# Layer 4's edges by tiles, and layer 3's node normalization three chunks ahead, in a four-layer graph network kernel

## The reference

```
# layer 3 (L2): message passing
h        = swish(concat(node[src], node[dst], edge_attr_32) @ We1 + be1)
agg      = segment_sum(h @ We2 + be2, dst) / 16
agg      = layernorm(agg) * g_msg + b_msg
nf       = swish(concat(node, agg) @ Wn1 + bn1) @ Wn2 + bn2
out      = layernorm(node + nf) * g_node + b_node

# layer 4 (L3): continuous filter convolution
C   = 0.5 * (cos(edge_weight * pi / 10) + 1)
W   = (ssp(edge_attr_50 @ mlp_w1.T + mlp_b1) @ mlp_w2.T + mlp_b2) * C[:, None]
msg = (x @ lin1_w.T)[src] * W
agg = segment_sum(msg, dst)
out = ssp(agg @ lin2_w.T + lin2_b)          # ssp(v) = softplus(v) - log 2
```

## Time and profile before

| | us |
|---|---|
| median of three runs | 9322.11 |
| profiled execution | 9326.77 |
| its span | 9325.0 |
| layer 3's edges, in the span | 4911 to 6950 |
| layer 3's nodes | 6950 to 7167 |
| layer 4's table | 7167 to 7213 |
| layer 4's edges | 7213 to 9277 |
| layer 4's nodes | 9277 to 9325 |

### The profile page before, as it was taken

The page is one execution under the profiler, slowest core; times in us unless marked ns, Lnnn a source line. Parts: engine busy times, 40 slices in busy tenths (PEclk is TensorE's granted clock), DMA queues, the critical chain, the costliest instruction groups (busy, mean ns, idle before and its releaser), DMA issues. The chain is left out here.

```text
span 9325.0 us, 221484 instructions
## 1 busy us (share of the span) xinstructions
PE 8295.5 (89%) x54969; PEld 6586.8 (71%) x54970; DVE 5838.0 (63%) x12428; ACT 5420.3 (58%) x14197; POOL 4943.9 (53%) x5229
## 2 busy tenths in 40 slices
PE   5999999989897999989988888888885999999998
PEld 4888888888884777766656666666663666666666
DVE  6888888888885777751145555555554555555555
ACT  5777777777774444430026767676754555555555
POOL 5666666666660000000007777777760777777775
PEclk8999999999998999999989999999997999999999
DMA  6888888888881222235544444444430222222222
GB/s 193 224 227 226 227 224 227 226 226 227 225 226 43 111 110 117 110 125 192 190 143 116 118 118 118 118 118 118 118 112 28 74 73 73 73 73 73 73 73 69
DMA packets 963534, 1294.60 MB, mean 139 GB/s; under 512 B 187018, under 2 KB 821186, under 8 KB 934210
## 3 DMA queue, kind: packets, MB, share of 16 engines
q1 hardware_dynamic: 769858, 837.45, 30.7%
q0 software_dynamic: 193536, 455.41, 17.7%
HBM read 906.61 MB, written 385.62 MB: 139 GB/s over the span
## 5 line engine op out<-in xcount | busy, mean ns | idle before, releaser
L1823 POOL DMA_INDIRECT x<-table,p_gidx x1632 | 1546.5, 948 | 2377.7 <-ACT p_gidx L1860 1957.9
L672 POOL DMA_INDIRECT g_G<-table,g_runs x1776 | 1686.5, 950 | 769.9 <-issue 479.5
L2275 POOL DMA_INDIRECT c_G<-table,c_gidx x1632 | 1548.4, 949 | 505.2 <-issue 497.1
L820 PE MATMUL g_ps_cell<-g_loh,g_kw 128*98 128x128 f32 x9472 | 1254.1, 277 | 29.2 <-DVE g_kw L743 29.2
L831 PE MATMUL g_ps_rev<-g_hrow,g_AT 128*128 128x129 f32 x7252 | 1054.6, 284 | 192.3 <-DMA g_AT<-turn_save 155.1
L820 PEld LDWEIGHTS g_ps_cell<-g_loh,g_kw 128*98 128x98 f32 x9472 | 1127.5, 168 | 29.7 <-DVE g_kw L743 29.4
L1913 PE MATMUL p_ps_sum<-x 128*96 128x256 f32 x3264 | 898.4, 398 | 231.5 <-DVE hid L1849 221.3
L798 ACT COPY g_X<-g_ps_cell 98x512 f32<-98x512 f32 x1184 | 681.4, 576 | 720.8 <-PE g_ps_cell L820 697.9
L831 PEld LDWEIGHTS g_ps_rev<-g_hrow,g_AT 128*128 128x128 f32 x7252 | 930.2, 197 | 239.9 <-issue 184.0
L1913 PEld LDWEIGHTS p_ps_sum<-x 128*96 128x96 f32 x3264 | 468.7, 163 | 646.0 <-ACT x L1878 260.3
L1849 DVE TENSOR_TENSOR hid<-hid,p_ps_sum 96x256 f32 x1632 | 678.0, 415 | 375.2 <-DVE hid L1849 372.1
(11 more groups left out here) (344 smaller groups left out, 15168.1 us busy)
## 6 DMA issues: line engine op xcount, KB each, us to landing
turn_save<-g_X SPq DMA_DIRECT2D x1184, 196.0 KB
g_AT<-turn_save SPq DMA_DIRECT2D x592, 392.0 KB
adj_save<-a_A SPq DMA_DIRECT2D x74, 1568.0 KB, 5.1
a_A<-adj_save SPq DMA_DIRECT2D x74, 1568.0 KB, 6.6
c_ed<-in_edge_dram SPq DMA_DIRECT2D x1632, 25.0 KB
g_G<-table,g_runs POOLq DMA_INDIRECT x1776
p_lhs<-in_edge_dram SPq DMA_DIRECT2D x1632, 16.0 KB
x<-table,p_gidx POOLq DMA_INDIRECT x1632
```

Of the source, the lines that this page charges most:

```text
L672: g.indirect_dma_start(G[:, e % GR, q, 0:D], None, table, bass.IndirectOffsetOnAxis(ap=runs[:, n % 2, 0, RQ * e + q:RQ * e + q + 1], axis= ...
L820: last = pe.matmul(ps_cell[q % 2][0:KEYS, r * P:(r + 1) * P], kw[:, b, cell, :], loh[:, b, cell, :], start=True, stop=True)
L1823: g.indirect_dma_start(G[:, H * b + q, :], None, table2, bass.IndirectOffsetOnAxis(ap=gidx[:, b, q:q + 1], axis=0)).then_inc(gathered[b], 16)
L2275: g.indirect_dma_start(G[:, H * b + q, :], None, table, bass.IndirectOffsetOnAxis(ap=gidx[:, b, q:q + 1], axis=0)).then_inc(gathered[b], 16)
```

## The change

In layer 4's edges the loop over pairs becomes straight-line code over 391 steps of four tiles, followed by sums of pairs: every tile is loaded, filtered and gathered once, in the order of the tiles, and only one-hots, sums and adds still go over 408 quads of pairs. The source indices come from a new input `src_cols` in one transfer of 128 x 1564 integers. `c_G` becomes a ring of 32 steps, from which PE picks a pair's tile at a slot that it computes in registers (`slots_of`). The one-hots are made up to 17 steps ahead, between the adds. The bias is cut into three bf16 parts and put into `c_ps_filt` by a bf16 product. ACT's three copies, the `top` matrix and the loop's bookkeeping go; `c_ps_filt` and `c_ps_sum` get three banks instead of two. The sums of step n wait for the messages of tile step min(n, 390).

In layer 3's nodes ACT's take_aggT and activate, and DVE's take_nf and measure_nf, come three chunks later in their streams (`LEAD`).

```diff
+LEAD = 3
+STEPS = NI * NB
+TSTEPS = -(-ET // H)
+RS = 32
+CES = 4
+COH = 18
...
-                        for c in range(NQ + 4):
+                        for c in range(NQ + 4 + LEAD):
...
-                            if 3 <= c < NQ + 3:
-                                take_nf(c - 3)
-                            if c >= 4:
-                                measure_nf(c - 4)
+                            if 3 + LEAD <= c < NQ + 3 + LEAD:
+                                take_nf(c - 3 - LEAD)
+                            if c >= 4 + LEAD:
+                                measure_nf(c - 4 - LEAD)
...
-                            if 1 <= c <= NQ:
-                                take_aggT(c - 1)
-                            if c >= 2:
-                                activate(c - 2)
+                            if 1 + LEAD <= c <= NQ + LEAD:
+                                take_aggT(c - 1 - LEAD)
+                            if c >= 2 + LEAD:
+                                activate(c - 2 - LEAD)
...
+                def slots_of(eng, n):
+
+                    word = eng.value_load(bucket_row[0:1, bass.ds(n, 1)])
+                    return [nc.s_assert_within(eng.snap((n * H + q + 2 * P - ((word >> (7 * q)) & 127)) & (RS * H - 1)), 0, RS * H - 1,
+                                               skip_runtime_bounds_check_because="masked to the ring") for q in range(H)]
...
+                        sp.dma_start(index[:, :], a["src_cols"]).then_inc(index_in, 16)
...
+                        for s in range(TSTEPS):
+                            if s >= CES:
+                                sp.wait_ge(linear, s - CES + 1)
+                            sp.dma_start(ed[0:DE3, s % CES, :], a["edge50"][:, s * CH:(s + 1) * CH]).then_inc(edges_in[s % CES], 16)
...
+                        for s in range(TSTEPS):
+
+                            if s >= RS:
+                                g.wait_ge(summed, (H * (s - RS) + H - 1 + NBK - 1) // H + 1)
                             for q in range(H):
-                                g.indirect_dma_start(G[:, H * b + q, :], None, table,
-                                                     bass.IndirectOffsetOnAxis(ap=gidx[:, b, q:q + 1], axis=0)).then_inc(gathered[b], 16)
...
+                                g.indirect_dma_start(G[:, s % RS * H + q, :], None, table,
+                                                     bass.IndirectOffsetOnAxis(ap=index[:, H * s + q:H * s + q + 1], axis=0)).then_inc(gathered[s % RS], 16)
...
+                        for n in range(STEPS + 2):
+                            bucket = buckets_of(v, n - 2) if n >= 2 else None
+                            if n < TSTEPS:
+                                messages(n)
+                            ahead = min(2 * n + 3, n + COH - 1, STEPS)
                             for q in range(H):
...
+                                if n >= 2:
+                                    add_up(n - 2, q, bucket)
+                                for m in range(made, ahead):
+                                    one_hot(m, q)
+                            made = ahead
...
+                        def filters(s):
+                            if s >= 3:
+                                pe.wait_ge(message, s - 2)
+                            pe.matmul(ps_filt[s % 3][:, :], one[:, :], shift[:, :, :].rearrange("p q d -> p (q d)"), start=True, stop=False)
+                            pe.wait_ge(act_step, 4 * s + 4)
...
+                        def make_sums(n, slot):
+                            if n >= 3:
+                                pe.wait_ge(added, H * (n - 2))
+                            pe.wait_ge(oh_ready, n + 1)
+                            pe.wait_ge(message, tile_step(n) + 1)
...
+                        line(0)
+                        for n in range(STEPS + 1):
+                            if n + 1 < TSTEPS:
+                                line(n + 1)
+                            slot = slots_of(pe, n - 1) if n >= 1 else None
+                            if n < TSTEPS:
+                                filters(n)
+                            if n >= 1:
+                                make_sums(n - 1, slot)
```

More of the change, by code:

```diff
@@ new lines, in messages, with add_up @@
+                        def messages(s):
+                            v.wait_ge(filtered, s + 1)
+                            v.wait_ge(gathered[s % RS], 16 * H * (s // RS + 1))
+                            here = G[:, s % RS * H:(s % RS + 1) * H, :]
+                            v.tensor_tensor(here, here, by_tile(ps_filt[s % 3][:, :]), ALU.mult).then_inc(message, 1)
+                        def add_up(n, q, bucket):
+                            at = bass.ds(bucket[q], 1)
+                            if q == 0:
+                                v.wait_ge(summed, n + 1)
+                            if n or q:
+                                v.wait_ge(added, H * n + q)
+                            v.tensor_tensor(acc[0:BN, at, :], acc[0:BN, at, :],
+                                            ps_sum[n % 3][0:BN, q * P:(q + 1) * P].rearrange("p (o d) -> p o d", o=1),
+                                            ALU.add).then_inc(added, 1)
@@ L2284, in _ @@
+                        v.memset(acc[:, :, :], 0.0).then_inc(acc_clear, 1)
                         v.wait_ge(loaded, 64)
-                        v.wait_ge(added, 2 * H)
-                        v.wait_ge(cleared, 5)
-                        v.memset(top[0:1, :], 1.0).then_inc(shift_ready, 1)
                         v.wait_ge(column_sums, 1)
-                        for q in range(H):
-                            last = v.scalar_tensor_tensor(out=shift[0:1, q, :], in0=ps_filt[0][0:1, 0:D], scalar=-LOG2, in1=b2[:, :],
-                                                          op0=ALU.mult, op1=ALU.add)
@@ L2307, in add_up @@
[L2307 to L2316, removed]
@@ new lines, in _ @@
+                        v.wait_ge(shift_step, 7)
+                        v.tensor_copy(cut[:, 2, :], exact[:, 2, :]).then_inc(shift_step, 1)
+                        v.wait_ge(shift_step, 8)
+                        v.scalar_tensor_tensor(out=row[:, :], in0=cut[:, 2, :], scalar=ident[:, 2:3], in1=row[:, :],
+                                               op0=ALU.mult, op1=ALU.add).then_inc(shift_step, 1)
+                        v.wait_ge(shift_step, 9)
+                        v.tensor_copy(shift[:, :, :], across(row[:, :])).then_inc(shift_step, 1)
@@ L2357, in line @@
-                        def line(i, b):
-                            n = NB * i + b
-                            pe.wait_ge(edges_in[b], 16 * H * (i + 1))
-                            if not (isinstance(n, int) and n < 2):
-                                pe.wait_ge(act_step, 4 * n - 6)
-                            pe.matmul(ps_lin[b % 2][:, :], w1[:, :], ed[:, b, :], start=True, stop=True).then_inc(linear, 1)
-                        def filters(i, b):
-                            n = NB * i + b
-                            pe.wait_ge(act_step, 4 * n + 4)
-                            pe.wait_ge(message, n + 1)
-                            pe.matmul(ps_filt[b % 2][:, :], top[:, :], shift[:, :, :].rearrange("p q d -> p (q d)"), start=True, stop=False)
+                        pe.wait_ge(shift_step, 10)
```

133 lines of the change are left out of this document (62 added, 71 removed).

## The result

The changed kernel takes 9212.7 us (median of four runs, 9210.4 to 9218.8) against 9321.0 us for the kernel before on the same chip: ratio 0.9888, 95% interval 0.9871 to 0.9905. The prediction was 9226 us in a range of 9200 to 9264. The profiled execution took 9218.77 us, its span 9217.0, which is 108.0 us under the span before.

The account below looks back on a forecast made before the run. It took POOL's gathers to bound layer 4's edges and waits between engines to hold up layer 3's nodes. Layer 4 at -46.9 us (-87.6 - 3.3 + 44.0) and layer 3 at -49.3 gave -96.2: 9226 us, range 9200 to 9264.

Parts of the forecast that it names:

- Bound: Layer 4 edges: POOL's gathers, 1.254 us each, set the step; 68 fewer, first to last gather -87.6 us.
- First gather: Layer 4 edges: it waits for one index load of 0.8 MB and starts 3.3 us earlier.
- PE's step: Layer 4 edges: 3.8 us of products plus about 1.0 us of registers, under the gathers' 5.02 us.
- Wholly unhidden: 4.8 us: Layer 4 edges: PE's step if none of its register work overlaps products, still under 5.02 us.
- Tail: End of layer 4: 20 steps of DVE adds at 2.42 us remain after the last message, +44.0 us.
- rival D: End of layer 4: the tail is PE's, 60 us or more, total 9237 us; 10 in 100.
- Layer 3's nodes: With the later take of nf PE becomes the bound, 4.98 us a chunk, stage -49.3 us.
- Clock: Layer 4 edges: despite PE idling some 1.2 us in 5, at most passing dips that the ring absorbs.
- rival B: Layer 4: the clock falls in most steps; at half of them total +170 us, 9492 us; 2 in 100.
- Rival A: Layer 4: PE becomes the bound at 5.5 us a step, total +103 us, 9425 us; 5 in 100.
- C: Layer 3's nodes keep most of their time through an unseen wait, -15 instead of -49, 9260 us; 7 in 100.
- E: Layer 4: the gathers' pace changes with more queued, +31 us, 9257 us; 4 in 100.

Follow-up runs that it names:

- l3_only: The kernel before with only the layer 3 nodes part of the change (LEAD = 3): 9267.1 us, ratio 0.9937 to the kernel before.
- l4_only: The changed kernel with LEAD = 0 in layer 3's nodes, so only the layer 4 part: 9275.6 us, ratio 0.9945 to the kernel before.
- ready_slots: The changed kernel with the sums' ring slots packed in advance, so PE only shifts and masks: 9237.5 us, ratio 0.9905 to the kernel before.
- shift_twice: The changed kernel with layer 4's shift product in fp32 instead of bf16 and issued twice: 9322.2 us (one run).

## Why the prediction was right

- **Bound.** POOL's gathers set the step before and after, as predicted: 0.30 us of "issue" ahead of each, fewer gathers, same pace. First to last was -95.3 us for -87.6. Of the 7.7 us, 2.4 to 5.2 are not the change's: the profiled execution of before had the slower gathers and that of after the faster ones. Between two with fast gathers (`l3_only` and the changed kernel) the change gives -90.0, and 2.4 are left, which is 1563 times 1.5 ns of shorter pace; between two with slow ones (before and `l4_only`) it gives -92.9.
- **First gather.** 4.46 us after the stage's first POOL instruction instead of 7.77: -3.3, as predicted.
- **PE's step.** Predicted 3.8 us of products; 3.73 measured, the bf16 shift product 0.22 for the 0.2 taken. The registers were mis-sized: the prediction added up the records' lengths, 0.17 us a tile, where the operations start 0.1 us apart and a tile takes 0.61; with the load that is 4 x 0.61 + 0.37 = 2.8 us a step of the sequencer, not 1.0. It did no harm, because they run beside products: neither 0.64 us more of products nor three more loads a step moved the gathers. "Wholly unhidden: 4.8 us" was the wrong way to bound the step; products alone and sequencer alone are the two things to bound.
- **Tail.** +49.9 us for +44.0. The mechanism was rival D's: "PE's next registers can run beside its matmuls" held, but was no reason for DVE's figure: a tile's two products take 0.43 us from start to start even at the lower clock, and its registers 0.61, so the registers set the pace. 18 sums steps at 2.86 us and the last adds stand in place of 20 steps of adds at 2.42. With ready slots the tail is 47.3, DVE's price. D's 60 us, products and registers in series, was too much. The step of the prediction that failed here is its choice of DVE as the tail's owner, and the total did not show it: the tail's +5.9 us were outweighed by gathers that were 7.7 us shorter than forecast, in part by which execution was profiled. That the two made up for each other is luck.
- **Layer 3's nodes.** -50.5 us for -49.3, chunk 4.92 us for 4.98, PE the bound, turns without a wait. The 2 us left out for an earlier hidden(0) came: 2.3.
- **Clock.** 1.00 in the steady part of layer 4 (rival B did not happen), although DVE and PE both have over 1 us to spare in a step; 0.50 in the tail. The passing dips that the prediction allowed for did come: four of them, 14 us in all, between 7500 and 9100 us (one lies in the window below), where the kernel before had none in its steady part; the gathers kept their pace. With `ready_slots` PE idles for DVE's adds ahead of the sums of 287 of some 320 steps between 7400 and 9000 us, 0.77 us on average, and the granted clock there is 1.00 as well. For long it fell only where the full steps ended. The case that the Trainium skill describes (TensorE: Matmul & The Clock Gate, "HAM oscillation — how this bites in real kernels") has bursts of products that are shorter than the waits for data between them. The prediction stretched it: here a step holds 3.7 us of products beside 1.3 us of room, and no steady part here has bursts shorter than its waits, so the traces neither confirm nor refute the page.

```profile
7530.00:7540.00 10.00, 8.41 (x42) 6.01 (x43) 6.27 (x22) 3.42 (x6) 7.56 (x9) 0.83 0.25 64
```

- **Rival A** needed 5.02 us of products or of issue; `shift_twice` shows what it would have looked like, and that the array gets there with 1.5 us more. C and E did not happen.
- **Sum.** Steps predicted -96.2, measured -100.9 (-50.5 - 2.3 - 3.3 - 95.3 + 49.9, and +0.6 between the last gather and the last message), and -7.1 from stages that were not touched: gathers of layer 3 4.3 us, the rest layers 1 and 2.

## What to carry over

Where TensorE computes addresses in registers between its matmuls, don't add registers to products: while products are queued the sequencer works ahead, and the step is set by the longer of the two; the registers show where only short products are left, as in a drain. When work is cut from the front of a pipeline whose later stage keeps its count, look at what is left at the end, and price it for each engine, register operations by the distance of their starts (0.1 us here) and not by the length of their records (0.03 to 0.05). And compare stages by their own marks before wholes: here the untouched layer 1 spread over 29 us.

## What the hardware showed that I had not expected

- An indirect gather of layer 4 lasts 944 to 949 ns on average, by the execution and by the code (949 and 946 in the old code, 946 and 944 in the new, slow and fast); executions with slower gathers were slower in layer 3 and layer 4 alike (2047 against 2043 us for 1632 gathers in layer 3).
- Three more register loads on PE's sequencer in each of 391 steps, about 1.1 us a step where they are uncovered, cost nothing in the steady part.
- PE's step in the changed kernel looked full (4.83 to 5.20 us with idle times below 0.3) while its array had 1.3 us to spare: records without large gaps say nothing of the room when issue is what stretches them.
- A register operation on PE's sequencer has a record of 29 to 46 ns and takes about 100 ns from start to start: 5.75 a tile fill 0.61 us, at 1.2 and 2.4 GHz alike, and 2.75 fill 0.32 at 2.4 GHz.
